# One pipeline over batches for perceptron, norms, router, shared expert and token placing, in a transformer block with a mixture of experts

## The reference

```python
x = L0_attn_hidden_states                       # 8 batches x 512 tokens x 128
h = _layernorm(x) * (1 + ca) + sa
x = x + ga * _L0_attn_ref(h, ...)               # attention, then a 512-wide perceptron
h = _layernorm(x) * (1 + cb) + sb
x = x + gb * _L0_ffn_ref(h, ...)

# in _L0_attn_ref, after attention
x2 = _layernorm(h, ln2_g, ln2_b)
hmid = gelu(x2 @ fc1_U @ fc1_V + fc1_b)
return h + hmid @ fc2_U @ fc2_V + fc2_b

# _L0_ffn_ref: 8 experts, the best 2 of each token
normed = hidden_states * rsqrt(mean(hidden_states**2) + 1e-08) * norm_weight
shared = maximum(normed @ sw1 + sb1, 0.0) @ sw2 + sb2
probs = sigmoid(flat @ router_w.T)
scores, idx = top_k(probs, 2)
w = scores / (sum(scores) + 1e-06)
# routed = sum over the 2 picks of w * (maximum(flat @ ew1[e] + eb1[e], 0) @ ew2[e] + eb2[e])
return shared + routed
```

## Time and profile before

| | us |
|---|---|
| median of 3 runs (906.5 to 907.08) | 906.88 |
| the profiled execution, its own time | 905.57 |
| its span, first to last instruction | 902.9 |
| `attend()` | 447.5 |
| `mlp()` | 115.5 |
| `route()` | 136.2 |
| `experts()` | 172.6 |
| `combine()` | 31.1 |

### The profile page before, as it was taken

How to read it: one execution, slowest core, us unless ns; L and a number is a source line. 1 busy time by engine, 2 the same in 40 slices (tenths; PEclk the granted TensorE clock), 3 DMA queues, 4 the chain that set the end, 5 groups by cost and what they waited for, 6 DMA issues and landing times. The chain is left out here.

```text
span 902.9 us, 15792 instructions
## 1 busy us (share of the span) xinstructions
PE 672.0 (74%) x5322; PEld 407.9 (45%) x5322; DVE 419.0 (46%) x1079; ACT 419.8 (46%) x733; POOL 312.9 (35%) x491
## 2 busy tenths in 40 slices
PE   4447999989899999998178885753328799999900
PEld 3213334433334433432146554433026699899900
DVE  1568887777775666661148763800003011111117
ACT  5120666656666665558255654311012355555513
POOL 2441323323332222121134432277730154455523
PEclk9999999999999999999679996985559799999965
DMA  8233323333333333112294111011100677778627
GB/s 178 83 111 128 110 81 127 99 111 106 122 100 125 105 124 106 47 48 76 67 271 92 46 47 61 30 55 51 51 27 0 184 226 215 223 208 227 187 87 207
DMA packets 104347, 102.68 MB, mean 114 GB/s; under 512 B 12912, under 2 KB 88600, under 8 KB 104192
## 3 DMA queue, kind: packets, MB, share of 16 engines
q1 hardware_dynamic: 95264, 89.12, 33.4%
q0 software_dynamic: 4544, 9.45, 3.0%
q10 hardware_dynamic: 4480, 3.35, 1.5%
HBM read 58.97 MB, written 38.72 MB: 108 GB/s over the span
## 5 line engine op out<-in xcount | busy, mean ns | idle before, releaser
L962 DVE TENSOR_REDUCE row_max<-ps_s 128x1 f32<-128x384 f32 (+3 forms) x384 | 216.2, 596 | 98.9 <-PE ps_s L722 75.8
L583 ACT ACTIVATE work<-ps_s 128x1024 f32<-128x1024 f32 (+1 forms) x192 | 168.5, 883 | 67.2 <-PE ps_s L751 64.7
L722 PE MATMUL ps_s<-k_st,q_st 128*128 128x384 bf16 (+3 forms) x512 | 129.2, 309 | 0.0
L1531 POOL DMA_INDIRECT y_d<-res,target x78 | 74.9, 960 | 124.5 <-DVE res L1596 109.5
L719 PE MATMUL ps_s<-later_q,ident_b 128*128 128x128 bf16 (+1 forms) x384 | 94.4, 250 | 17.2 <-DVE row_max L962 13.8
L768 PE MATMUL ps_pv<-work,v_sb 128*32 128x512 f32 (+3 forms) x1024 | 95.5, 446 | 1.3 <-ACT ctx_raw L617 1.2
L719 PEld LDWEIGHTS ps_s<-later_q,ident_b 128*128 128x128 bf16 x384 | 37.2, 98 | 113.2 <-DVE row_max L962 78.9
L1596 DVE TENSOR_TENSOR res<-ps_s,bias 128x256 f32<-128x256 f32 x39 | 16.6, 425 | 137.1 <-PE ps_s L1583 134.2
L1583 PEld LDWEIGHTS ps_s<-w_tile,x_hidden 128*128 128x128 f32 x624 | 75.6, 192 | 2.0
L1573 PE MATMUL ps_s<-tok_t,w_tile 128*128 128x256 f32 x312 | 76.2, 388 | 0.0
L1583 PE MATMUL ps_s<-w_tile,x_hidden 128*128 128x128 f32 x624 | 75.8, 275 | 0.0
(11 more groups left out here) (198 smaller groups left out, 1028.4 us busy)
## 6 DMA issues: line engine op xcount, KB each, us to landing
w_tile<-in_ew SPq DMA_DIRECT2D x39, 514.0 KB
ctx_d<-ctx_raw SPq DMA_DIRECT2D x32, 256.0 KB, 3.0
q_st<-q_d SPq DMA_DIRECT2D x64, 102.0 KB
k_st<-k_d SPq DMA_DIRECT2D x64, 96.0 KB
slots_d<-fill SPq DMA_DIRECT2D x1, 5148.0 KB, 23.1
rows<-slots_d SPq DMA_DIRECT2D x39, 132.0 KB
got<-y_d SPq DMA_DIRECT2D x16, 256.0 KB, 3.2
q_d<-qk_part SPq DMA_DIRECT2D x8, 384.0 KB, 2.7
```

What stands on the lines that cost most here:

```text
L583: act.activation(dst, src, ACT.Exp, scale=SCALE).then_inc(exp_done, 1)
L722: mm = pe.matmul(bnk[:, k * keys:(k + 1) * keys], q_st[b % 2][:, g, j, i * P:(i + 1) * P], k_st[b % 2][:, g, j // 2, 0:keys], start=False, ...
L962: dve.reduce_max(row_max[:, m % 2, js[0] % 2, j:j + len(js), i], src, AXIS.X).then_inc(max_taken, 1)
L1531: pool.indirect_dma_start(y_d[:], bass.IndirectOffsetOnAxis(ap=target[:, k, c:c + 1], axis=0), res[:, k, c, :], None).then_inc(put[k], 16)
```

## The change

`mlp()` and `route()` become one block, `dense()`, with all loops written out. Its steps n run from -1 to 11, and each does something for batches n+1 to n-4. Each expert now has a fixed region of 17 x 256 slots, so a pick's slot needs only the counts of the batches before (kept in `seen`), and batch b is placed as soon as it is routed. `tile_row` tells `experts()` where each tile's rows stand. The weight of a pick is written into the token's row (two copies, `n3x[:, 0]` and `n3x[:, 1]`) and multiplied on DVE in `experts()`, so `combine()` only adds, gates and adds, four buffers deep, with ACT and POOL doing no arithmetic. fc1 and the shared expert's first layer share three PSUM banks in a fixed order (`RING`). `fill` has 30 columns of rows instead of 78.

The order of the work on each engine is what matters, and it is this:

```diff
+def rstd_of(k, b, moments_ready, eps_added, root, shifted):        # POOL, three operations
+    pool.tensor_tensor(var_eps[:, k, :], moments[:, k, m, :, 1], ln_eps[:], ALU.add)
+    pool.tensor_tensor(rstd[:, k, m, :], var_eps[:, k, :], half_neg[:], ALU.pow)
+    pool.tensor_tensor(shift[:, k, m, :], neg_mean[:, k, m, :], rstd[:, k, m, :], ALU.mult)
+def scatter(b):
+    pool.wait_ge(slots_ready, b + 1)
+    pool.wait_ge(n3_copied, 16 * (b + 1))
+    for c in range(2):
+        for i in range(NT * b, NT * (b + 1)):
+            pool.indirect_dma_start(slots_d[:], ...slots[:, c, i:i + 1]..., n3x[:, c, i, :], None)
+for n in range(-1, B + 4):                                         # POOL
+    if has(n - 1): rstd_of(1, n - 1, x_moments, x_eps, x_rstd, x_shift)
+    if has(n + 1): rstd_of(0, n + 1, h_moments, h_eps, h_rstd, h_shift)
+    if has(n - 1): rms_of(n - 1)
+    if has(n + 1): bias_h(n + 1)
+    if has(n - 2): scatter(n - 2)
+for n in range(-1, B + 4):                                         # ACT
+    if has(n - 1): x_hat_of(n - 1)          # 4 x 128x128, waits for x_shift
+    if has(n):     gelu(n)
+    if has(n - 1): squares(n - 1)           # waits for h3_steps
+    if has(n + 1): normalise(n + 1)         # 4 x 128x128, waits for h_shift
+    if has(n - 1): n3_of(n - 1) ... n3_t    # waits for n3_rstd, n3t_done
+    if has(n + 1): x2_t                     # waits for xt_done
+    if has(n - 1) and n >= B: exp_scores(n - 1)
+    if has(n - 3): relu(n - 3)
+    if has(n - 1) and n < B: exp_scores(n - 1)
+for n in range(-1, B + 4):                                         # PE
+    if has(n):     fc1(n)
+    if has(n - 4): l2(n - 4, 0)             # shared expert, second layer, first half
+    if has(n - 2): counts(n - 2)            # waits for chosen_ready
+    if has(n):     fc2(n)
+    if has(n - 1): transpose_n3(n - 1)      # waits for n3_ready
+    if has(n + 1): transpose_x(n + 1)
+    if has(n - 4): l2(n - 4, 1)
+    if has(n - 1): router(n - 1)            # waits for slots_ready, n - 1 batches
+    if has(n - 3): l1(n - 3)
+    if n - 2 == B - 1: all_counts()
+for n in range(-1, B + 4):                                         # DVE
+    if has(n - 1): h3_of(n - 1)             # 2 x 128x512
+    if has(n - 2): pick_two(n - 2)          # 14 small operations, waits for exped
+    if has(n + 1): norm_stats(0, h_sb, n + 1, h_stats, h_moments)
+    if has(n - 2) and n >= B: place(n - 2)
+    if has(n - 4): gate_shared(n - 4)       # 3 x 128x512, waits for l2_done
+    if has(n - 2) and n < B: place(n - 2)   # 11 small ones to slots_ready, waits for counted
+    if n - 2 == B - 1: map_tiles()
+    if has(n):
+        gate_mlp(n)                         # 3 x 128x512, waits for fc2_done
+        norm_stats(1, x_sb, n, x_stats, x_moments)
+    if has(n - 1): cap_logits(n - 1)
+for b in range(B):                                                 # SP
+    sp.dma_start(n3x[:, 1, NT * b:NT * (b + 1), 0:D], n3x[:, 0, NT * b:NT * (b + 1), 0:D])
+sp.wait_ge(fill_known, 1)
+for e in range(E):
+    at = sp.value_load(fill_at[0:1, e:e + 1], ...)
+    sp.dma_start(slots_d[bass.ds(at, SLOTS), :]..., fill[...])
...
 def experts():
-    sp.dma_start(rows[:, k], slots_r[:, bass.ds(t, 1), :, :]...)
+    row = sp.value_load(tile_row[0:1, bass.ds(t, 1)], ...)
+    sp.dma_start(rows[:, k], slots_r[:, bass.ds(row, 1), :, :]...)
...
-    dve.tensor_tensor(res[:, k], ps_s1[...], bias2[...], ALU.add).then_inc(res_ready, 1)
+    dve.tensor_tensor(biased[:], ps_s1[...], bias2[...], ALU.add).then_inc(bias_added, 1)
+    dve.wait_ge(bias_added, t + 1)
+    for c in range(HALVES):
+        dve.tensor_scalar(res[:, k, c], biased[:, c], rows[:, k, c, D + 1:D + 2], None, ALU.mult).then_inc(res_ready, 1)
...
 def combine():
+    DEEP = 4
-    act.activation(weighted[:, 0, k, i], got[:, 0, k, i], ACT.Copy, scale=picked_w[...])
-    pool.tensor_tensor(weighted[:, 1, k], got[:, 1, k], weight_of(1, b), ALU.mult)
-    dve.tensor_tensor(weighted[:, 0, k], weighted[:, 0, k], weighted[:, 1, k], ALU.add)
+    dve.tensor_tensor(routed[:, k], got[:, k, 0], got[:, k, 1], ALU.add)
+    dve.tensor_tensor(routed[:, k], routed[:, k], gate_b[:, b:b + 1, :].to_broadcast([P, NT, D]), ALU.mult)
+    dve.tensor_tensor(routed[:, k], routed[:, k], h_sb[:, NT * b:NT * (b + 1), :], ALU.add)
```

## The result

The changed kernel took 920.07 us (median of 4 runs, 917.49 to 923.56), the kernel before 906.69 beside it (4 runs): a ratio of 1.0168, 95% interval 1.0139 to 1.0197. It is slower, as forecast, but by 13.4 us where 5.6 were forecast. The profiled execution took 923.56 with a span of 921.8.

The account below looks back on a forecast made before the run. No engine but PE in `experts()` was nearly full; `route()` was a serial chain on POOL, the new block a ring of waits. +8.3 +1.6 -4.2 = +5.7 us gave 912.5 against 906.88; range 894 to 932.

Parts of the forecast that it names:

- The ring: In `dense()`, waits through POOL, ACT, DVE and PE set the time between scatter bursts: 260 us, +8.3.
- the long steps: Steps of `dense()` that wait for the shared expert's second layer: 33 us each, bounds 31 and 36.
- the ramp ahead of the first burst: Start of `dense()`, normalising and routing the first batches: first scatter at 50.4 us.
- the tail behind the last one's start: End of `dense()`, from the eighth burst at 240.5 us until PE's remaining work and the last gate end at 260.
- rival 3: PE at 1.2 GHz throughout `dense()`: steps of 35.6 instead of 33, +18 us, 930 in all; chance 0.12.
- the stall: In the old `route()`, the shared expert stops during POOL's indirect DMAs: DVE waits 59.3 us, 28 us left over.
- The failed step: In `experts()`, DVE's two products a tile and SP's extra register load would be mostly hidden: +1.6 us, bounds 0 and 3.
- Combine: In `combine()`, DMA work plus the first landing and DVE's last batch: 26.9 us, -4.2, bounds -9 and 0.
- a drain at each table load: The skill's 1.38 us per table switch on ACT in `dense()`: six reloads add 8.3, giving 921; not in the sum.
- Rival 1: In `dense()`, the shared expert's second layer does not hold the full steps: they stay at 24 us, 877; chance 0.15.
- Rival 2: At the end of `dense()`, PE's results are released only at POOL's drain: about +15 us, 928; chance 0.14.
- Rival 4: In `dense()`, ACT empties before each of six table loads, 0.68 us each: +4, 917; chance 0.06.

Follow-up runs that it names:

- c2: The kernel before, unchanged, run and profiled again in a later set where it is short: 875.17 us in the profiled execution.
- c3: The changed kernel, unchanged, run once more in a set where the kernel before is short: 911.75 us, ratio 1.0424.
- b1: The changed kernel with DVE's placing of a batch ahead of `gate_shared` in the full steps too: `dense()` took 222.8 us.
- a5: The changed kernel with eight instead of four buffers for rows, weights and biases of the experts' tiles: `experts()` took 167.0 us.
- a3: The changed kernel with the row number read before SP's wait and DVE's products with the pick weights left out: `experts()` took 171.5 us.

## Why the forecast was right in sign and wrong in size

- **The ring: right.** 260.7 for 260, and each milestone of the step within 1 us. Parts of it cancelled: the long steps were 31.2 to 31.5 in the middle, the lower bound of 31 rather than the 33 that had some slow PE in it (fc2, 3.82, and half of l2, 1.95, ran at the full clock there), while the ramp ahead of the first burst was 52.1 instead of 50.4 and the tail behind the last one's start 22.8 instead of 19.5, with 2.9 of late release in it. The layout has four long steps; its bounds and rival 3 counted five. And +8.3 met +9.0 against a `route()` that happened to have the stall: against c2 the same block is 32 longer.
- **The failed step: the experts.** "DVE gets two 128x128 products a tile ... far under PE's: nothing but at the last tile", and "SP loads one more register before the first rows ... every later load hidden by four buffers", +1.6, bounds 0 and 3. Both counted engine time. Both lie on the path from a result to SP's next issue, 0.53 and 0.66 us in nearly every tile, and that path had no room for them: +14.1 (+14.3 between c3 and c2). DVE's operations were sized well (0.48 for the pair). The mistake was to take cover for granted: no row was sought for how long before PE's need a tile's rows landed. Between 740 and 850 us the kernel before already had PE waiting for rows in five places, 0.9 us at most: the reserve was used up. In c2 no such wait stands between 717 and 827 us, so there was some reserve there, but less than the 1.2 us added.
- **Combine: right mechanism, mis-sized.** -7.0 for -4.2. DMA's work was 0.92 x 24.1 = 22.2 (21.5 forecast); the 3 us ahead and 2.2 behind it were counted in full and lay mostly beside it. (The three terms add up to 26.7, not 26.9.)
- **Sum.** +9.0 +14.1 -7.0 +2.8 = +18.9 in the spans, +13.4 in the medians: the profiled execution of the changed kernel lies 3.5 above its median, that of the kernel before 1.1 below. That the measured 920.07 lies next to the 921 that the forecast gave with a drain at each table load is chance: no drain is there, and the excess is in `experts()`.
- **Rival 1** (the hold by l2 does not bind, 877) fell: the hold binds, 7.4 us a step. Lifting it by one moved line (b1) gives steps of 24.1, its number. **Rival 2**: one late release of 2.9 us at the end instead of 15, and none in c3. **Rival 3**: the block's clock was 0.77, but the steps' PE pieces in the ring were at full speed. **Rival 4**: out, by the table loads above.
- **What the forecast had not considered:** that the stall, the very thing that the change hides, comes and goes by itself. Where it is away, `route()` is 26 us shorter, and the change costs 4.2% instead of 1.7%.

## What to carry to other kernels

When an edit puts an operation between a result and the issue of the next load, count it on the path of the buffer, not on the engine: release, register load, issue, landing, against the time until the consumer wants it; deeper load buffers (a5) were worth more than either saving alone. In a pipeline with hand-written orders, walk the ring through all engines, then look for the one line whose move shortens it: `place` ahead of `gate_shared` gave 34 to 38 us for nothing. And profile the kernel before more than once before a stall in it is taken as something to be won.

## What was unexpected of the hardware

- During POOL's unbroken stream of indirect DMAs PE's matmuls can come singly, 1.4 to 2.8 us apart, and a result can be taken up 41 us after its last matmul (one wait of 59.3 us). This is absent in other sets of the same kernel, 905 against 874 us, and with pauses behind every eighth DVE's waits were 10.0 at most.
- SP's load of one register from SBUF costs 0.66 us between its wait and its DMA issue; read ahead of the wait it adds nothing between the two in the median tile (0.65 in a3 as in c2).
- Two activation tables taking turns cost 1.28 us a load and at most 0.02 more on either side when the next activation is ready, also when ACT comes straight from an activation.
